# Per-channel attention kernel on one core: twelve e buffers, later column sums, halved T and y products, new order of loads and of the prologue

## Chip, cores, metric

One core of a Trainium2 chip (trn2) runs the whole program. The metric is the device time of one execution in microseconds (us).

## The reference, cut to what matters

x has the shape (8, 256, 32, 16): batch element, row, channel, column m. C_H is 256.

```python
n = group_norm(x)            # 8 groups over m (2 columns each); mean and variance over rows, channels, the group's columns
Q, K, V = W @ n + b          # over channels, for each (b, row, m): 32 -> 256; all stored as (B, S, 256, M)
QK = Q^T @ K                 # per (b, m): 256 x 256, summed over the 256 rows
A = softmax(QK, axis=-1)
out = einsum('bmcC,bmsC->bsCm', A, Vp)   # V weighted by the column sums of A
y = x + Wo @ out + bo
```

In the last einsum the letter c occurs only in A, so only the column sums of the softmax are needed: `a[C] = sum over c of A[c, C]`. And Q^T K depends on x only through the 32 x 32 Gram matrix of each (b, m) and the column sums of x.

## The kernel before

**Work.** An element is one b; it has 16 units m = 4t + q, four groups t of four units q. For an element the chain of statistics is: sums of rows (`sum_rows`, L361), group means (`mean`, L374), the rows centred on GpSimd (L910), the Gram matrix (`gram_of`, L382), the variance (`variance`, L400), the scaled Gram matrix `gnorm` (GpSimd, L941), its product with Wk for all four t (`t_product`, L410: 16 matmul calls into `bz` for even t and `by` for odd t) and with the bias (`tb_product`, L430), read out by VectorE (`read_t` L640, `read_tb` L651), split into a high and a low part (GpSimd L962, L985) and copied by DMA into `stack` (SyncE, L302).

**Softmax.** For each unit, TensorE computes a 256 x 256 score (`score`, L438: two halves into one of the four PSUM banks `s_bank`), VectorE the negated row maximum (`maximum`, L663), ScalarE two exponentials of 256 columns, each with its row sum (`exponentials`, L849), into one of `NE` = 8 buffers `e_sb`. After the four units of a group VectorE inverts the row sums (`invert`, L669) and TensorE adds the weighted columns into `acc` (`column_sums`, L454, in two halves h, 4 calls each). With 8 buffers ScalarE may begin group n + 2 only when the column sums of group n are done (L853).

**Output.** When an element's 16 units are done, `acc` is read (L673), turned into columns (`a_columns`, L468, bank `bx`; `read_a`, L678), multiplied into the output weights (GpSimd L997; `weights`, L479, bank `by`; `read_weights` and `read_bias`), and one element later `y_product` (L497: 16 calls into `bz` and `by`) is read by ScalarE (`read_even`, L860: two activations) and VectorE (`read_odd`, L699) and stored by SyncE (L325).

**Order.** The program is written in slots: slot 16b + p belongs to unit p of element b. Every engine runs its list in order, and waits are semaphores. In slot p TensorE first issues the score three units ahead (L536), VectorE the maximum two units ahead, ScalarE the exponentials of the unit itself. The column sums of group n stand at slots 4n + 5 and 4n + 6 (L542). The tables `ANCHOR`, `CHAIN`, `EARLY` (L42 to L52) place the statistics of element j, `OUT`, `OUT_FIRST`, `OUT_LAST` (L55 to L61) the output of the elements before. For element 5 on, seen from element b = j - 3 or j - 2: sum_rows slot 0, mean 3, Gram matrix 8, variance 13, then in the next element T product 3, its four reads 4 to 7, bias product 8 and its read 9. Weights stand at slot 13, their read at 15, the y product at 11 and its reads at 12. `BUSY` (L63) and `keep_busy` (L518, 4 calls a round) fill TensorE with products whose results nobody reads.

**Prologue** (L564 to L592, L787 to L821, L879 to L895, L1011 to L1034). SyncE loads the rows of elements 0 to 3, 512 KB each. ScalarE's queue loads the constants `k_sb` first, then Wk, the later constants `k2_sb`, bk, the stacked Wq, bv, bo, Wo and Wv; seven of these count on one semaphore, `w_loaded`, and the first T product (L577) and the splitting of Wq (L969) wait for all seven. `sum_rows` takes its matrix of ones from `k_sb`. Elements 0 and 1 are begun outside the slots; the first half of element 0's `stack` is copied as soon as t = 0 and 1 are split.

Of the kernel before, what the change touches and what calls it, by code (L numbers as in the profile page):

```python
# [8 lines left out]
CH = 256  # L9
G = 8  # L10
P = 128
# [15 lines left out]
ONES = PICK + M  # L27
LOMASK = ONES + C
# [13 lines left out]
ANCHOR = {2: 7, 3: 22, 4: 36, **{j: M * (j - 2) + 3 for j in range(5, B)}}  # L42
CHAIN = dict(
    sum_rows=-19, mean=-16, gram=-11, variance=-6, t_product=0, tb_product=5,
    sum_groups=-18, read_mean=-15, read_gram=-9, sum_diagonal=-8, read_variance=-5,
    read_t0=1, read_t1=2, read_t2=3, read_t3=4, read_tb=6,
)
EARLY = {
    2: {**CHAIN, **dict(gram=-7, variance=-4, read_gram=-6, sum_diagonal=-5, read_variance=-3)},
    3: {**CHAIN, **dict(sum_rows=-17, mean=-14, gram=-10, sum_groups=-16, read_mean=-13)},  # L50
    4: {**CHAIN, **dict(sum_rows=-18, mean=-15, sum_groups=-17, read_mean=-14)},
# [3 lines left out]
OUT = dict(read_acc=3, a_columns=5, read_a=6, weights=13, read_weights=15,  # L55
           y_product=11, read_even=12, read_odd=12)
OUT_FIRST = {**OUT, **dict(a_columns=7, read_a=8)}

OUT_LAST = dict(read_acc=3, a_columns=4, read_a=5, weights=8, read_weights=10,
                y_product=1, read_even=2, read_odd=3,  # L60
                y_second=12, read_even_second=13, read_odd_second=13)  # L61

BUSY = {(1, 3): 1, (1, 5): 1, (B - 1, 1): 2, (B - 1, 5): 2, (B - 1, 6): 1, (B - 1, 9): 1}  # L63
# [10 lines left out]
def shape_constants():  # L74
# [10 lines left out]
    k[:, ONES:ONES + C] = 1.0  # L85
# [15 lines left out]
def build(nc, x_rows, x_cols, wq_stack, wk_rep, bk_rep, wv, wo, bv, bo_rep, consts, later, y_cols):  # L101
# [7 lines left out]
    NE = 2 * Q  # L109
# [4 lines left out]
    with ctx:  # L114
# [23 lines left out]
        half = sb("half", [P, T])  # L138

# [43 lines left out]
        k_loaded = sem("k_loaded")  # L183
        k2_loaded = sem("k2_loaded")
# [31 lines left out]
        t_mm = sem("t_mm")  # L216
# [24 lines left out]
        y_mm = sem("y_mm")  # L241
        even_read = sem("even_read")
# [7 lines left out]
        def rows_of(eng, j):  # L250
            eng.wait_ge(xs_loaded[j], 16)
            return xs[:, j]
# [10 lines left out]
        def odd_t_bank(j):  # L263
            return {0: s_bank[0], 1: acc}.get(j, by)

        def odd_y_bank(j):
            return bx if j == B - 1 else by
# [21 lines left out]
        ones_m = k_sb[:, ONES:ONES + C]  # L289
# [5 lines left out]
        def _(sp):  # L295
# [29 lines left out]
            def store(j):  # L325
                sp.wait_ge(even_read, j + 1)
# [3 lines left out]
            for j in range(4):  # L330
                load_rows(j)
# [28 lines left out]
        def _(pe):  # L360
# [39 lines left out]
            def variance(j):  # L400
                pe.wait_ge(gram_done, j + 1)
                pe.wait_ge(trace_done, j + 1)
                if j == 0:
                    pe.wait_ge(k2_loaded, 16)
# [686 lines left out]
```

## Time and profile before

| | us |
|---|---|
| median of 3 runs (lowest, highest) | 184.82 (183.56, 187.84) |
| the profiled execution, its own time | 183.17 |
| its span, first to last instruction | 181.4 |
| busy: TensorE matmuls, VectorE, ScalarE, GpSimd | 153.9, 129.3, 127.9, 99.9 |
| mean granted TensorE clock | 0.979 of 2.4 GHz |

PE is TensorE, PEld its loading of weights, DVE VectorE, ACT ScalarE, POOL GpSimd, SP SyncE. L numbers are lines of the kernel before. Matmul ends are modelled, so a busy PE is not PE at its peak; intervals from start to start are firmer. One fp32 matmul call shows as two MATMUL records. The profiled execution is 1.65 us faster than the median of the three runs.

### The profile page before, as it was taken

What the parts mean: (1) busy time and instruction counts of PE and PEld (TensorE: products, weight loads), DVE (VectorE), ACT (ScalarE), POOL (GpSimd) and SP (SyncE); (2) the same over time, 40 slices, a digit from 0 to 9 for tenths busy, and PEclk for the clock granted to TensorE, in tenths of its full rate; (3) what the DMA queues carried; (4) which work ended last, traced back from release to release, by engine and by line L of the source; (5) the groups of instructions that cost most, each with busy time, mean ns of one, the idle gap of its engine ahead of it and who ended that gap; (6) DMA issues with size and microseconds to landing.
All of it is one profiled execution on the core that took longest, in us unless ns stands there. A gap on an engine that the chain in (4) does not pass through costs nothing. (4 is left out here: it accounts for less than half of the span.)

```text
span 181.4 us, 6452 instructions
## 1 busy us (share of the span) xinstructions
PE 153.9 (85%) x2448; PEld 87.1 (48%) x2448; DVE 129.3 (71%) x297; ACT 127.9 (71%) x529; POOL 99.9 (55%) x130
## 2 busy tenths in 40 slices
PE   6879797999978998899898979788978889899590
PEld 2254454555444655465545545544443445554340
DVE  0466899597778689767986798679778676668231
ACT  0200059789976798789688968897999998979301
POOL 3247739459975997685867595764742405125000
PEclk9996998799999999999999999999999999999999
DMA  5940859873992588099808870797077821200203
GB/s 179 409 157 4 202 150 176 187 241 54 206 226 114 101 213 268 21 176 230 301 5 160 193 243 4 129 215 250 4 150 169 264 90 41 116 4 5 116 4 116
DMA packets 10540, 26.72 MB, mean 147 GB/s; under 512 B 2603, under 2 KB 4110, under 8 KB 10510
## 3 DMA queue, kind: packets, MB, share of 16 engines
q1 hardware_dynamic: 8734, 25.25, 52.7%
q10 hardware_dynamic: 1776, 1.05, 2.0%
q8 instruction: 20, 0.33, 0.8%
q14 instruction: 10, 0.08, 0.2%
HBM read 9.13 MB, written 4.19 MB: 73 GB/s over the span
## 5 line engine op out<-in xcount | busy, mean ns | idle before, releaser
L855 ACT ACTIVATE e_sb<-s_bank,negmax 128x256 f32<-128x256 f32 x256 | 117.4, 491 | 33.9 <-DVE negmax L665 18.1
L665 DVE TENSOR_REDUCE negmax<-s_bank 128x2 f32<-128x512 f32 x128 | 85.8, 683 | 17.9 <-PE s_bank L450 16.6
L450 PE MATMUL s_bank<-stack,wq_st 99*128 99x256 f32 x256 | 57.3, 322 | 4.4 <-ACT e_sb L855 4.2
L855 ACT ACTIVATION_READ_ACCUMULATOR e_sb<-s_bank,negmax 128x1 f32 x256 | 57.3, 224 | 0.0
L450 PEld LDWEIGHTS s_bank<-stack,wq_st 99*128 99x128 f32 x256 | 37.0, 190 | 35.5 <-issue 35.1
L462 PE MATMUL acc<-e_sb,recip 128*32 128x256 f32 x512 | 41.4, 398 | 13.2 <-DVE recip L671 13.1
L462 PEld LDWEIGHTS acc<-e_sb,recip 128*32 128x32 f32 x512 | 10.6, 109 | 24.4 <-DVE recip L671 18.7
L1000 POOL TENSOR_TENSOR ws<-wo_sb,aT 128x1024 f32<-128x1024 f32 x7 | 13.4, 1910 | 13.5 <-DVE aT L681 13.5
L987 POOL TENSOR_TENSOR t_parts<-t_sb,t_parts 128x1280 fp32r<-128x1280 f32 x7 | 20.4, 2913 | 0.5
L916 POOL TENSOR_TENSOR xc<-xs,nm 128x512 f32<-128x512 f32 x12 | 12.3, 1043 | 7.4 <-DVE nm L619 7.4
L994 POOL TENSOR_TENSOR xcT<-xT,nmT 128x1024 f32<-128x1024 f32 x8 | 15.1, 1892 | 0.0
L865 ACT ACTIVATE yb<-bz,beff 128x256 f32<-128x256 f32 x16 | 6.7, 473 | 10.4 <-PE bx L514 7.6
L647 DVE SCALAR_TENSOR_TENSOR t_sb<-bk_sb,ssum,bz 128x256 f32<-128x256 f32 x16 | 7.6, 474 | 5.4 <-PE by L426 3.6
L939 POOL TENSOR_TENSOR rs<-vare,half 128x4 f32<-128x4 f32 x8 | 8.2, 1022 | 5.8 <-DVE vare L637 5.8
L1008 POOL TENSOR_TENSOR wf<-wn,k_sb 128x128 f32<-128x128 f32 x7 | 3.2, 455 | 14.8 <-DVE wn L688 14.8
L424 PE MATMUL bz<-wk_sb,gnorm 32*32 32x256 f32 x128 | 9.4, 406 | 0.5 <-DMA wv_sb<-wv 0.5
L933 POOL TENSOR_TENSOR gdiag<-gram,k_sb 128x128 f32<-128x128 f32 x6 | 2.6, 436 | 13.1 <-DVE gram L624 13.1
L512 PE MATMUL bz<-xcT,wf 32*32 32x256 f32 x128 | 8.7, 380 | 0.3 <-issue 0.3
L965 POOL CAST t_parts<-t_sb 128x1280 fp32r<-128x1280 f32 x6 | 7.5, 1250 | 2.0 <-DVE t_sb L654 2.0
L671 DVE RECIPROCAL recip<-rowsum 128x8 f32<-128x8 f32 x32 | 6.2, 194 | 2.1 <-ACT e_sb L855 2.1
L514 PE MATMUL by<-xcT,wf 32*32 32x256 f32 x112 | 7.6, 380 | 0.0
L609 DVE TENSOR_REDUCE part<-bx 128x4 f32<-128x256 f32 x7 | 2.8, 398 | 6.5 <-PE bx L369 6.4
(99 smaller groups left out, 180.9 us busy)
## 6 DMA issues: line engine op xcount, KB each, us to landing
stack<-t_parts SPq DMA_DIRECT2D x28, 256.0 KB, 5.0
stack<-t_parts SPq DMA_DIRECT2D x36, 128.0 KB, 4.6
xs<-x_rows SPq DMA_DIRECT2D x8, 512.0 KB, 5.4
xT<-x_cols SPq DMA_DIRECT2D x8, 512.0 KB, 5.5
y_cols<-yb SPq DMA_DIRECT2D x7, 512.0 KB, 3.6
y_cols<-yb SPq DMA_DIRECT2D x2, 256.0 KB, 2.6
stack<-t_parts ACTq DMA_DIRECT2D x4, 64.0 KB, 3.0
stack<-t_parts SPq DMA_DIRECT2D x4, 64.0 KB, 2.4
```

Source lines behind the costliest of these rows:

```text
L424: nc.tensor.matmul(bz[rows, cols], gnorm[rows, j % 2, 2 * i, :], wk_sb[rows, :], start=True, stop=True)
L450: mm = nc.tensor.matmul(s_bank[p % NS][:, CH * h:CH * h + CH], wq_st[:, P * h:P * h + P], stack[:, side, p % Q, p // Q, :], start=True, st ...
L462: mm = nc.tensor.matmul(acc[C * q:C * q + C, 0:CH], recip[:, t, q, h, :], e_sb[:, (Q * t + q) % NE, h, :], start=(t == 0 and h == 0), stop ...
L512: nc.tensor.matmul(bz[rows, cols], wf[rows, j % 2, 2 * i, :], xcT[rows, j % 2, 2 * i, :], start=True, stop=True)
L514: mm = nc.tensor.matmul(odd[across(q), cols], wf[rows, j % 2, 2 * i + 1, :], xcT[rows, j % 2, 2 * i + 1, :], start=True, stop=True)
L665: nc.vector.tensor_reduce(negmax[:, p % NS, :], s_bank[p % NS][:, :].rearrange("p (h n) -> p h n", h=HC), op=ALU.max, axis=AX.X, negate=Tr ...
L855: last = nc.scalar.activation(e_sb[:, p % NE, h, :], s_bank[p % NS][:, CH * h:CH * h + CH], ACT.Exp, bias=negmax[:, p % NS, h:h + 1], accu ...
L916: last = nc.gpsimd.tensor_tensor(xc[:, ch, :, 0:C].rearrange("p (g k) c -> p g k c", g=G), src[:, ch, :, :].rearrange("p (g k) c -> p g k ...
L939: nc.gpsimd.tensor_tensor(rs[:, j, :], vare[:, 0:T], half[:, :], ALU.pow).then_inc(rs_done, 1)
L987: nc.gpsimd.tensor_tensor(t_parts[:, j % 2, 1], t_sb[:, j % 2], t_parts[:, j % 2, 0].bitcast(f32), ALU.subtract).then_inc(parts_done, 1)
L994: nc.gpsimd.tensor_tensor(xcT[:, j % 2], xT[:, j], nmT[:, j, :, None].to_broadcast([P, T, S]), ALU.add).then_inc(xcT_done, 1)
L1000: nc.gpsimd.tensor_tensor(ws[:, :, :, :, :].rearrange("p h t q c -> p h (t q) c"), wo_sb[:, :, None, :].to_broadcast([P, HC, M, C]), aT[:, ...
```

## The change

- Twelve buffers `e_sb` (`NE` = 3Q), three sets of row sums; ScalarE waits at group n + 3 for the column sums of group n.
- The column sums of group n stand at slots 4n + 6 and 4n + 7.
- The T product and the y product are issued in halves (t = 0, 1 and t = 2, 3; 8 calls each) in neighbouring slots: T at slots 4 and 5, its reads at 6 (t = 1), 7 (t = 3), 8 (t = 0), 9 (t = 2), the bias product at 9 (it waits for two of the four reads only), its read at 11; y's first half at slot 13 with ScalarE's first read at 14, its second half at slot 0 of the next element, with ScalarE's second read at slot 1 and VectorE's at 2. In the last element they stand at slots 4, 5 and 12, 13.
- The weights (matmuls of L486 and L493) go to `bx`, the bank of the statistics and of `a`, at slot 12 with the read at 13; they wait for the read of the Gram matrix of element j + 4 instead of bank `by`. `variance` moves to 14, its read to 15, `sum_rows` to 1, `mean` to 4; in the element of the variance it waits for the bias read.
- `BUSY`: four rounds at slots 1, 2, 3 and 5 of element 0 are added (bank `by`); in the last element four rounds instead of six.
- Loads: the ones come from a memset. SyncE loads half of element 0's rows, then `k_sb`; ScalarE loads the other half, Wk, stacked Wq, `k2_sb`, bk and then the rest, with semaphores of their own for `k_sb`, Wk, Wq and bk. `w_loaded` counts the last four and is waited for by the product of Wo and bv and the first `a_columns`.
- Prologue: 3 rounds of `keep_busy` before the first `sum_rows`, which waits for the rows alone; T of element 0 in halves into four banks, the second half after the Gram matrix of element 1, with 6 rounds of `keep_busy` around where 3 were; `split_wq` before the first `power`.

```diff
-ANCHOR = {2: 7, 3: 22, 4: 36, **{j: M * (j - 2) + 3 for j in range(5, B)}}
+ANCHOR = {2: 8, 3: 22, 4: 36, **{j: M * (j - 2) + 4 for j in range(5, B)}}
-    sum_rows=-19, mean=-16, gram=-11, variance=-6, t_product=0, tb_product=5,
+    sum_rows=-19, mean=-16, gram=-12, variance=-6, t01_product=0, t23_product=1, tb_product=5,
-    read_t0=1, read_t1=2, read_t2=3, read_t3=4, read_tb=6,
+    read_t1=2, read_t3=3, read_t0=4, read_t2=5, read_tb=7,
...
-OUT = dict(read_acc=3, a_columns=5, read_a=6, weights=13, read_weights=15,
-           y_product=11, read_even=12, read_odd=12)
+OUT = dict(read_acc=4, a_columns=5, read_a=6, weights=12, read_weights=13,
+           y01_product=13, read_y0=14)
+OUT_NEXT = dict(y23_product=0, read_y2=1, read_odd=2)
...
-BUSY = {(1, 3): 1, (1, 5): 1, (B - 1, 1): 2, (B - 1, 5): 2, (B - 1, 6): 1, (B - 1, 9): 1}
+BUSY = {(0, 1): 1, (0, 2): 1, (0, 3): 1, (0, 5): 1, (1, 3): 1, (1, 5): 1,
+        (B - 1, 3): 1, (B - 1, 8): 1, (B - 1, 9): 1, (B - 1, 11): 1}
...
-    NE = 2 * Q
+    NE = 3 * Q
...
-            for j in range(4):
+            sp.dma_start(xs[:, 0, 0], x_rows[0, :, 0]).then_inc(xs_loaded[0], 16)
+            sp.dma_start(k_sb[:, :], consts).then_inc(k_loaded, 16)
+            for j in range(1, 4):
                 load_rows(j)
...
-                    pe.wait_ge(t_read, T * (j + 1))
+
+                    pe.wait_ge(t_read, T * j + 2)
...
-                    if slot >= Q + 1 and p % Q in (1, 2):
-                        n = (slot - Q - 1) // Q
-                        column_sums(n // T, n % T, p % Q - 1)
+                    if slot >= Q + 2 and p % Q in (2, 3):
+                        n = (slot - Q - 2) // Q
+                        column_sums(n // T, n % T, p % Q - 2)
...
-            keep_busy(s_bank[3], t_sb[:, 0, T, :], 4)
+            keep_busy(s_bank[3], t_sb[:, 0, T, :], 3)
+            sum_rows(0)
             pe.wait_ge(k_loaded, 16)
-            sum_rows(0)
...
-            pe.wait_ge(w_loaded, 16 * 7)
-            t_product(0)
+            pe.wait_ge(wk_loaded, 16)
+            t_product(0, 0, t01_mm)
+            keep_busy(s_bank[3], wk_sb, 1)
             tb_product(0)
             gram_of(1)
-            keep_busy(s_bank[3], wk_sb, 2)
+            t_product(0, 2, t23_mm)
+            keep_busy(s_bank[3], wk_sb, 3)
             variance(1)
             mean(2)
-            keep_busy(s_bank[3], wk_sb, 1)
-            t_product(1)
+            keep_busy(s_bank[3], wk_sb, 2)
+            t_product(1, 0, t01_mm)
+            t_product(1, 2, t23_mm)
...
                 if p % Q == 0:
-                    after(act, summed, T * b + p // Q - 1)
+                    after(act, summed, T * b + p // Q - NE // Q + 1)
...
-            act.dma_start(k_sb[:, :], consts).then_inc(k_loaded, 16)
-            act.dma_start(wk_sb[:, :], wk_rep).then_inc(w_loaded, 16)
+            act.dma_start(xs[:, 0, 1], x_rows[0, :, 1]).then_inc(xs_loaded[0], 16)
+            act.dma_start(wk_sb[:, :], wk_rep).then_inc(wk_loaded, 16)
+            act.dma_start(wq_raw[:, :], wq_stack).then_inc(wq_loaded, 16)
             act.dma_start(k2_sb[:, :], later).then_inc(k2_loaded, 16)
-            for dst, src in ((bk_sb, bk_rep), (wq_raw, wq_stack),
-                             (bv_sb, bv), (bo_sb, bo_rep)):
+            act.dma_start(bk_sb[:, :], bk_rep).then_inc(bk_loaded, 16)
+            for dst, src in ((bv_sb, bv), (bo_sb, bo_rep)):
                 act.dma_start(dst[:, :], src).then_inc(w_loaded, 16)
```

## Rows read from the trace of the kernel before

**Rows 1.** The page, part 1: busy us of each engine over the span

```profile
PE 153.9 (85%) x2448; PEld 87.1 (48%) x2448; DVE 129.3 (71%) x297; ACT 127.9 (71%) x529; POOL 99.9 (55%) x130
```

**Rows 2.** Windows per element: us; busy PE, PEld, DVE, ACT, POOL; granted clock; DMA share

```profile
23.55:42.34 18.79, 17.17 (x277) 9.85 (x277) 16.11 (x36) 15.15 (x64) 10.38 (x19) 0.91 0.69 171
42.34:61.27 18.93, 16.41 (x264) 9.84 (x263) 14.01 (x33) 15.23 (x64) 14.84 (x17) 1.00 0.65 148
61.27:79.97 18.70, 16.97 (x283) 10.33 (x283) 15.13 (x38) 15.85 (x67) 15.04 (x18) 1.00 0.68 162
79.97:98.53 18.56, 16.50 (x279) 9.97 (x279) 14.99 (x37) 15.85 (x67) 13.23 (x17) 1.00 0.68 174
98.53:117.10 18.57, 16.52 (x279) 9.97 (x279) 14.99 (x37) 15.85 (x66) 13.23 (x17) 1.00 0.61 146
117.10:134.49 17.39, 14.64 (x199) 8.08 (x199) 14.03 (x32) 15.71 (x67) 9.72 (x11) 1.00 0.64 155
134.49:150.84 16.35, 13.36 (x165) 7.53 (x165) 12.36 (x27) 15.63 (x67) 4.21 (x3) 1.00 0.60 175
150.84:168.24 17.40, 16.05 (x240) 8.34 (x239) 11.91 (x27) 15.40 (x65) 6.52 (x5) 1.00 0.08 32
```

**Rows 3.** Waits over the whole span: us in total, times, longest

```profile
ACT e_sb L855 <- PE acc L462: 15.7, 23, 1.4
PE acc L462 <- DVE recip L671: 13.1, 23, 1.9
```

**Rows 4.** Timeline of ACT: the first exponential of two units in a row

```profile
67.16 0.48 ACT L855 ACTIVATE e_sb<-s_bank,negmax 128x256 f32<-128x256 f32 x1
...
68.06 0.50 ACT L855 ACTIVATE e_sb<-s_bank,negmax 128x256 f32<-128x256 f32 x1
```

**Rows 5.** Timeline of PE in elements 4 and 5: start, us, records

```profile
108.14 0.38 PE L435 MATMUL by<-wk_sb,sblk 128*32 128x256 f32 x1 [0.18 <-DVE t_sb L647]
108.28 0.26 PE L395 MATMUL bx<-xc 128*32 128x33 f32 x6
...
109.24 0.50 PE L450 MATMUL s_bank<-stack,wq_st 99*128 99x256 f32 x2
109.68 0.64 PE L462 MATMUL acc<-e_sb,recip 128*32 128x256 f32 x8
110.25 0.50 PE L450 MATMUL s_bank<-stack,wq_st 99*128 99x256 f32 x2
...
111.68 0.40 PE L512 MATMUL bz<-xcT,wf 32*32 32x256 f32 x1
...
112.70 0.74 PE L450 MATMUL s_bank<-stack,wq_st 99*128 99x256 f32 x4
114.34 0.64 PE L462 MATMUL acc<-e_sb,recip 128*32 128x256 f32 x8 [0.89 <-DVE recip L671]
...
120.90 0.40 PE L424 MATMUL bz<-wk_sb,gnorm 32*32 32x256 f32 x1
...
126.30 0.59 PE L435 MATMUL by<-wk_sb,sblk 128*32 128x256 f32 x2 [0.19 <-DVE t_sb L647]
126.82 0.51 PE L450 MATMUL s_bank<-stack,wq_st 99*128 99x256 f32 x2
```

**Rows 6.** Timeline of the prologue

```profile
5.20 1.08 PE L369 MATMUL bx<-xs,k_sb 128*32 128x256 f32 x8 [0.19 <-DMA k_sb<-consts]
...
13.24 0.45 PE L424 MATMUL bz<-wk_sb,gnorm 32*32 32x256 f32 x1 [0.51 <-DMA wv_sb<-wv]
...
13.69 0.19 POOL L955 TENSOR_TENSOR ssum<-vare,rs 128x2 f32<-128x2 f32 x1
...
15.18 0.48 DVE L647 SCALAR_TENSOR_TENSOR t_sb<-bk_sb,ssum,bz 128x256 f32<-128x256 f32 x1 [1.50 <-PE s_bank L426]
```

**Rows 7.** A window of the prologue, with the columns of rows 2

```profile
12.00:16.00 4.00, 3.40 (x59) 1.45 (x61) 2.46 (x6) 0.00 (x0) 3.57 (x7) 0.68 0.01 4
```

**Rows 8.** Timeline of POOL in element 4: the power behind the statistics of element 7

```profile
116.33 1.02 POOL L939 TENSOR_TENSOR rs<-vare,half 128x4 f32<-128x4 f32 x1 [0.96 <-DVE vare L637]
```

More of the change, by code:

```diff
@@ L26 @@
 PICK = MEAN + 2 * P
[L27 to L28 removed]
+LOMASK = PICK + M
 OWN = LOMASK + 1
@@ L351, in _ @@
             store(B - 2)
-            for h, done in ((1, odd_read), (0, even_read)):
+            for h, done in ((1, odd_read), (0, y2_read)):
                 sp.wait_ge(done, B)
@@ L408, in variance, with t_product @@
                                  ).then_inc(var_mm, 1)
-            def t_product(j):
+            def t_product(j, first, done):
                 pe.wait_ge(gnorm_done, j + 1)
@@ L413, in t_product @@
                 after(pe, tb_done, j)
[L414 to L415 removed]
+                after(pe, y2_read, j - 4)
                 after(pe, odd_read, j - 4)
[L417 to L418 removed]
+                if j == 1:
                     pe.wait_ge(vare_done, 2)
[L420 to L428 removed]
+                even, odd, cols = t_bank(j, first), t_bank(j, first + 1), t_cols(j, first)
+                for q in range(Q):
+                    rows = slice(C * q, C * q + C)
+                    nc.tensor.matmul(even[rows, cols], gnorm[rows, j % 2, first, :], wk_sb[rows, :],
+                                     start=True, stop=True)
+                    mm = nc.tensor.matmul(odd[across(q), cols], gnorm[rows, j % 2, first + 1, :], wk_sb[rows, :],
+                                          start=True, stop=True)
+                mm.then_inc(done, 1)
             def tb_product(j):
@@ new lines, in element @@
+                    if (j := due("mean", slot)) is not None:
+                        mean(j)
+                    if last and p == at["y01_product"]:
+                        y_product(b - 2, 0, y01_mm)
+                    if last and p == at["y23_product"]:
+                        y_product(b - 2, 2, y23_mm)
+                    if (j := due("t01_product", slot)) is not None:
+                        t_product(j, 0, t01_mm)
+                    if (j := due("t23_product", slot)) is not None:
+                        t_product(j, 2, t23_mm)
@@ L640, in read_t @@
             def read_t(j, t):
-                dve.wait_ge(t_mm, j + 1)
+                dve.wait_ge(t01_mm if j == 0 and t < 2 else t23_mm, j + 1)
                 dve.wait_ge(ssum_done, j + 1)
@@ L746, in element @@
                         read_bias(b - 1)
-                    if b >= 2 and p == at["read_odd"]:
+                    if (j := due("read_variance", slot)) is not None:
+                        read_variance(j)
+                    if last and p == at["read_odd"]:
                         read_odd(b - 2)
```

216 lines of the change are left out of this document (109 added, 107 removed).

## Prediction

> **What bounds the kernel now.** I read the page first: no engine is busy all the time, and TensorE stands first with 153.9 us of a span of 181.4 [rows 1]. Then the span in one window per element [rows 2]: the eight elements take 144.7 us of it, the prologue before them 23.55 and the tail after the last exponential's start 13.2. In the elements the reader is to see three loads close together. ScalarE issues one unit (two exponentials with their row sums) every 0.90 us when nothing stops it [rows 4], 14.4 us for 16 units, and with the two reads of y (0.42 us each from start to start, an estimate from ScalarE's busy time of 15.85 against 15.23 without them) 15.3. TensorE is busy 16.5 us of 18.57 in elements 3 and 4, VectorE 15.0. Neither fills the element. The waits say why [rows 3]: ScalarE waits 15.7 us in 23 pieces for the column sums, and the column sums wait 13.1 us in 23 pieces for the inverted row sums, which come from ScalarE. That is a ring: with eight e buffers, group n + 2 may not begin before the column sums of group n, and these stand on TensorE two slots ahead of it, behind one score and whatever else the slot holds. When a slot holds a whole T or y product, the ring opens late. TensorE's in-order list waits in it too, so what it did not do then is late afterwards.
>
> So the present bound is the ring; behind it stands TensorE at 16.5, and behind that ScalarE at 15.3.
>
> **The change part by part.** Times are against the profiled execution (183.17, its span 181.4 and 1.8 around it).
>
> *Buffers and later column sums.* With twelve buffers the exponentials of group n + 3 wait for column sums that stand five slots earlier, at 0.9 us a slot 4.5 us ahead instead of 1.8. The longest wait there was 1.4 us [rows 3], so I take all 15.7 us of ScalarE's waits as gone. And the column sums, a slot later, find their reciprocals ready: the longest wait of PE was 1.9 us with 0.9 typical [rows 3, 5], one slot more and the loss of the ring cover it. What is late next is TensorE's own work, so this part gives an element not 18.57 - 15.3 but at most 18.57 - 16.5 = 2.05 us.
>
> *What the halves and new slots cost TensorE.* A score followed by other work takes 0.44 us from start to start (109.24 to 109.68), two in a row busy it 0.74 where two apart take 0.88; a half of the column sums takes 0.57; the whole y product 1.02 (111.68 to 112.70) [rows 5]. Half of 1.02 would be 0.51; the nearest group that stands between two scores, the half of the column sums, costs 0.57. So two halves cost 1.14, 0.12 more, for T as for y: 0.24. The bias product and the Gram matrix stood in one slot and took 1.10 together (108.14 to 109.24); apart they take 0.52 (126.30 to 126.82) and 0.96 (108.28 to 109.24), so 0.38 more. Four slots of a steady element held a score alone and now none does: four times 0.07, 0.3. The weights and the variance no longer stand in one slot: 0.1. Sum 1.0 us, bounds 0 (TensorE hides it all) and 1.8 (twice the halves and the separations, as the nearest groups show no such case). So a steady element needs 16.5 + 1.0 = 17.5 us of TensorE, and TensorE becomes the bound.
>
> The rule that speaks against the halves is in the Trainium skill, "TensorEngine Tiling (Array Packing)", section "Key Properties": "Changing tiling mode (not just tile) drains the TensorE". The scores use 99 x 128 weights, the others 32 x 32 or 128 x 32, so each of three new seams (in T, in y, between bias product and Gram matrix) brings two more changes. If only they cost something, at the 0.07 us by which a lone score is dearer than one of a pair [rows 5], the six come to 0.4 us an element in the place of 1.0, and the time to 172.5.
>
> *Element by element* [rows 2]. I add 0.25 us for waits that remain (a guess between 0 and the 2.05 of now), where TensorE bounds.
> - Element 0: 18.79. Four added rounds of matmuls at 0.57 are 2.3 us, of which PE's idle 1.6 covers most; the low clock in it (0.91 on average) may go (up to 1.7 us of work saved) or stay. I take half: 18.3, gain 0.5.
> - Element 1: 16.41 busy, plus the halves of T, lone scores and separations 0.8, plus 0.25: 17.5, gain 1.45.
> - Element 2: 16.97 busy; y's second half leaves it (-0.5), +1.0 + 0.25: 17.7, gain 1.0.
> - Elements 3 and 4: 17.8, gain 0.75 each.
> - Element 5: TensorE needs 14.64 + 0.6 = 15.2, so ScalarE's 15.3 + 0.3: gain 1.8.
> - Element 6: 15.3 + 0.2, gain 0.85.
> - Element 7 (to the start of its last exponential): 16.05 busy, two rounds fewer (-1.1), y's half from before (+0.57), halves of two products (+0.25), a little wait: 16.2, gain 1.2. ScalarE there: 15 intervals of 0.90 and five reads, 15.6.
>
> Sum of gains 8.3 us. Edits I cost at nothing: the weights in `bx` at slot 12 (GpSimd has its products for them early in the element, it waits for the next step in between); the statistics' waits moved by a slot; VectorE's 15.0 us lie under 17.5, but leave only 0.3 under ScalarE's pace in elements that reach it; ScalarE's read of y at slot 14 must wait for a product issued one slot before, up to 1 us, which it makes good at 0.90 us a unit against TensorE's 1.1. SyncE's copies of `stack` for element b + 2 are issued more than half an element before they are needed; only those for element 1 have less, as element 0 gets shorter, and they move with the prologue.
>
> *Prologue.* The first product waited for `k_sb` until 5.20 [rows 6]; now it needs the rows alone, which come as the first load on both queues with half of the bytes on each. An estimate: 0.6 us earlier (0 to 0.9). The first T product waited 0.5 us for the last weight (to 13.24), and its first read (15.18) 1.5 us for all 16 calls, most of them at the low clock, 0.68 in that window [rows 6, 7]. The read also needs `ssum`, done at 13.88 [rows 6]; with the first half read by itself it can start right there. So this path ends 1.3 us earlier, plus the 0.6: 1.9. Against that the later constants and bk now lie behind more bytes on their queue, and the second half of T of element 0 comes later on. From the first split the SyncE queue is the bound up to the first scores, which moves as a whole; but the first score also stands behind element 1's bias product, whose chain gains the 0.6 and some of the rest. I take 1.6; bounds -0.5 (the later constants arrive last and the clock stays low) and 2.4.
>
> *Tail.* The last y product in halves: +0.12 for TensorE, while ScalarE reads one part early. VectorE's read of both odd parts is what the stores wait for, so 0 (bounds -0.4, +0.4).
>
> Sum: 183.17 - 8.3 - 1.6 = 173.3 against the profiled execution. The median of three runs stands 1.65 above that, so 174.9 on the scale of the runs.
>
> **The rivals.**
> 1. *The halves are free* (or the low clock goes for good): TensorE stays at 16.5 in elements 1 to 4, four times 1.0 us more gain and another 0.7 from element 0: about 170. For: matmul records overlap heavily. Against: a score alone takes 0.44, in a pair 0.37, and the bias product alone 0.52 [rows 5].
> 2. *ScalarE's pace everywhere*: if TensorE's busy time is no floor at all, elements 0 to 4 come to about 15.4: 18.2 us gained there in the place of 4.5, and 161 to 163. The rows speak against it: between waits TensorE's groups start back to back at 1.00 us for a score and half a column sum [rows 5], and these alone are 8 of the 16.5. A sentence of the Trainium skill speaks for it, in "Trainium Kernel Development and Optimization", section "Performance Expectations": matmul busy time is called a bad metric for the distance to the roofline, since matmuls are pipelined.
> 3. *The ring goes, but an in-order wait takes its place*: TensorE waits in slots 4, 5, 8 or 14, where three groups stand in a slot and VectorE's or ScalarE's part comes one slot behind it. If half of the 2.05 us of idle time stays, elements 1 to 4 give 0.8 us less each and 5 to 7 half of theirs, 1.9: 174.9 + 3.2 + 1.9 = 180.
> 4. *Slower*: T is read two slots later (11 instead of 9), so GpSimd's split of it (1.25 + 2.9 us) ends later and with it the power behind the next variance, the scaled Gram matrix and the T product at slot 4. Now the power starts at 116.33 [rows 8] and the T product at 120.90 [rows 5]; the power and two scalings fill about 1.6 us of that, so 3 us are free, and one slot has been added to T's place. If the delay came to more than 3 us, TensorE would stand still at slot 4 of five elements; each us beyond costs 5 us in all, and from 2 us beyond the whole gain is gone: with 2.5 beyond, 174.9 + 12.5 = 187. Against it: GpSimd waited 0.96 us for the variance in the row itself [rows 8], and is busy 13.2 of 18.6.
>
> **How the numbers follow.** My sum 0.56 (172.5 to 178), rival 1 0.13, rival 2 0.03, rival 3 0.23, rival 4 0.05. The range 168.5 to 181.0 leaves out rival 2, rival 4 and the far end of rival 3, some 2 in 10. A measurement of this kernel tells about 2% from no change, here 181.1: my sum, rivals 1 and 2 and two thirds of rival 3 lie under it, 0.88; within 2% 0.08; slower 0.04.
>
> **What would show it.** In the waits, the line of ScalarE waiting for the column sums should be under 2 us, and that of the column sums for the reciprocals under 4. In windows by element, elements 3 and 4 should take 17.3 to 18.0 with PE busy over 17, elements 5 and 6 near 15.5. The first exponential should start near 22.0. If elements 3 and 4 come to 16.5 or less, the cost of the halves is wrong; if they stay above 18.2 with TensorE idle over 1 us, rival 3 holds, and the waits name the place; if TensorE waits for `gnorm` at the T product, rival 4.

## The result and the profile after

The changed kernel took 180.99 us in the median of four runs (178.03 to 183.55), the kernel before 184.61 beside it. The ratio is 0.967, with a 95% interval of 0.959 to 0.976: faster by 3.3%, where I forecast 5.4% against 184.8. It compares the fast runs alone, 178.03 and 178.43 against three of the kernel before between 183.56 and 184.82; the medians of all runs are 2.0% apart. The median lies 0.01 us under the top of my range (181.0), and two of the four runs lie above the range: that the number fell inside is luck.

The profiled execution took 183.55 us, its span is 181.5, and it is one of those with a long stretch in which TensorE was granted half its clock. Busy times and idle time of the main groups, from the page (line, operation, count, busy us, mean ns, idle before and what ended it):

```profile
PE 167.0 (92%) x2480; PEld 88.7 (49%) x2480; DVE 130.1 (72%) x297; ACT 129.1 (71%) x529; POOL 100.1 (55%) x131
...
L880 ACT ACTIVATE e_sb<-s_bank,negmax 128x256 f32<-128x256 f32 x256 | 117.5, 497 | 22.1 <-DVE negmax L692 21.9
...
L475 PE MATMUL acc<-e_sb,recip 128*32 128x256 f32 x512 | 43.8, 419 | 0.8 <-DVE recip L698 0.8
```

ScalarE's 15.7 us of waiting for the column sums [rows 3] are gone, and the column sums wait 0.8 us for reciprocals where it was 13.1. The windows by element, with the prologue last, answer to [rows 2]:

```profile
core 0: us, PE busy (x) PEld busy (x) DVE busy (x) ACT busy (x) POOL busy (x), PEclk, DMA share, GB/s
23.83:40.84 17.01, 17.01 (x292) 9.14 (x291) 15.20 (x34) 15.27 (x64) 9.27 (x18) 1.00 0.75 192
40.84:59.15 18.31, 17.53 (x276) 10.30 (x275) 14.79 (x37) 15.63 (x64) 13.63 (x16) 1.00 0.60 148
59.15:76.53 17.38, 16.83 (x263) 9.41 (x263) 14.89 (x35) 15.57 (x65) 16.13 (x18) 1.00 0.69 166
76.53:94.10 17.57, 17.57 (x280) 9.69 (x280) 15.04 (x35) 15.99 (x68) 13.29 (x17) 1.00 0.71 184
94.10:111.66 17.56, 17.56 (x280) 9.69 (x280) 15.04 (x35) 15.99 (x68) 13.29 (x17) 1.00 0.64 156
111.66:127.66 16.00, 15.60 (x205) 8.17 (x204) 13.96 (x31) 15.53 (x69) 9.91 (x12) 1.00 0.67 165
127.66:146.39 18.73, 18.03 (x163) 9.33 (x162) 12.39 (x25) 15.51 (x68) 5.67 (x5) 0.68 0.55 139
146.39:168.01 21.62, 20.60 (x248) 9.49 (x248) 12.54 (x26) 16.33 (x68) 6.11 (x4) 0.81 0.13 50
...
0.00:23.83 23.83, 18.86 (x348) 9.97 (x348) 12.46 (x35) 1.28 (x2) 12.77 (x30) 0.93 0.59 188
```

What is to be seen: elements 3 and 4 take 17.57 and 17.56 us (18.56 and 18.57 before), and TensorE is busy in all of it. Elements 6 and 7 are longer than before, at a granted clock of 0.68 and 0.81. And the prologue is no shorter. Windows inside elements 6 and 7 show when the clock fell:

```profile
127.60:131.00 3.40, 3.18 (x39) 1.40 (x39) 2.72 (x6) 3.40 (x16) 2.92 (x3) 1.00 0.92 195
131.00:134.30 3.30, 2.86 (x24) 1.95 (x28) 3.17 (x9) 3.30 (x17) 0.52 (x2) 1.00 0.96 211
134.30:138.00 3.70, 3.70 (x23) 1.88 (x17) 1.68 (x3) 3.70 (x18) 1.83 (x1) 0.50 0.97 282
...
150.00:154.80 4.80, 4.80 (x38) 2.04 (x30) 2.56 (x5) 4.12 (x17) 1.89 (x1) 0.50 0.29 113
```

From 134.3 to 154.8 us TensorE ran at 1.2 GHz. The fall comes 6.6 us into element 6, which has the least work for TensorE (163 records against 280 in element 4).

The prologue, TensorE's first products:

```profile
4.17 0.81 PE L383 MATMUL bx<-xs,ones 128*32 128x256 f32 x8
8.47 1.08 PE L383 MATMUL acc<-xs,ones 128*32 128x256 f32 x8 [2.31 <-DMA xs<-x_rows]
10.49 1.08 PE L409 MATMUL bx<-xc 128*32 128x33 f32 x64
...
14.13 0.40 PE L436 MATMUL bz<-wk_sb,gnorm 32*32 32x256 f32 x1
```

The first row sums start at 4.17 instead of 5.20 [rows 6], as meant. But then TensorE waits 2.31 us for the rows of element 1, which its list wants before element 0's Gram matrix, and the first T product starts at 14.13 instead of 13.24. During that wait the granted clock fell to half, from 8.0 to 11.4 us: the row sums and the Gram matrix behind it took 1.08 us each, where 0.64 and 0.76 are their times at full rate.

### The profile page after: what moved, and what is told of

The parts are those of the page before. It is cut to its first block and busy times, and to the rows that moved or that the text cites. A ratio compares the mean times of both kernels' runs of the same rounds, so it can differ in the third digit from the quotient of the medians.

```text
span 181.5 us, 6548 instructions
## 1 busy us (share of the span) xinstructions
PE 167.0 (92%) x2480; PEld 88.7 (49%) x2480; DVE 130.1 (72%) x297; ACT 129.1 (71%) x529; POOL 100.1 (55%) x131
## 5 line engine op out<-in xcount | busy, mean ns | idle before, releaser
L692 DVE TENSOR_REDUCE negmax<-s_bank 128x2 f32<-128x512 f32 x128 | 87.0, 686 | 23.8 <-PE s_bank L463 22.8
L463 PE MATMUL s_bank<-stack,wq_st 99*128 99x256 f32 x256 | 64.7, 343 | 1.1 <-ACT e_sb L880 1.0
L463 PEld LDWEIGHTS s_bank<-stack,wq_st 99*128 99x128 f32 x256 | 40.2, 201 | 43.2 <-issue 42.3
L880 ACT ACTIVATION_READ_ACCUMULATOR e_sb<-s_bank,negmax 128x1 f32 x256 | 58.6, 229 | 0.0
L475 PE MATMUL acc<-e_sb,recip 128*32 128x256 f32 x512 | 43.8, 419 | 0.8 <-DVE recip L698 0.8
L475 PEld LDWEIGHTS acc<-e_sb,recip 128*32 128x32 f32 x512 | 10.7, 111 | 10.8 <-issue 1.8
L522 PE MATMUL bz<-xcT,wf 32*32 32x256 f32 x128 | 11.3, 415 | 1.8 <-ACT yb L889 1.8
L524 PE MATMUL by<-xcT,wf 32*32 32x256 f32 x128 | 11.4, 417 | 0.0
L533 PE MATMUL s_bank<-wk_sb 32*32 32x256 f32 x128 | 8.7, 379 | 0.0
L438 PE MATMUL by<-wk_sb,gnorm 32*32 32x256 f32 x96 | 7.9, 386 | 0.0
L730 DVE TENSOR_TENSOR yb<-by,beff 128x512 f32<-128x512 f32 x8 | 5.5, 683 | 3.3 <-PE by L524 3.3
```

Of the source, the lines that this page charges most:

```text
L463: mm = nc.tensor.matmul(s_bank[p % NS][:, CH * h:CH * h + CH], wq_st[:, P * h:P * h + P], stack[:, side, p % Q, p // Q, :], start=True, st ...
L475: mm = nc.tensor.matmul(acc[C * q:C * q + C, 0:CH], recip[:, t, q, h, :], e_sb[:, (M * b + Q * t + q) % NE, h, :], start=(t == 0 and h == ...
L522: nc.tensor.matmul(bz[rows, cols], wf[rows, j % 2, first, :], xcT[rows, j % 2, first, :], start=True, stop=True)
L524: mm = nc.tensor.matmul(by[across(q), cols], wf[rows, j % 2, first + 1, :], xcT[rows, j % 2, first + 1, :], start=True, stop=True)
L533: nc.tensor.matmul(dst[rows, 0:CH], src[rows, 0:C], src[rows, 0:CH], start=True, stop=True)
L692: nc.vector.tensor_reduce(negmax[:, p % NS, :], s_bank[p % NS][:, :].rearrange("p (h n) -> p h n", h=HC), op=ALU.max, axis=AX.X, negate=Tr ...
```

## The experiments

Where elements are compared, it is in profiles in which their clock is full. The kernel before ran beside them between 181.3 and 203.0 us, with granted clocks from 0.995 down to 0.839, so times of single variants say less than their windows do.

**1. The changed kernel again.** No edit.

> The changed kernel once more. Theory A (the ring is gone, TensorE bounds elements 2 to 4, and what the last two elements lost comes from a half clock in them): elements 3 and 4 take 17.5 to 17.6 us whatever the clock does later, and the spread of the runs (178.0 to 183.6) is the length of the low-clock stretch in elements 6 and 7. A profile with a short stretch shows element 7 shorter and elements 0 to 5 the same within 0.3 us. Rival (the spread comes from the loads or the prologue): the first exponential's start moves by as much as the whole time does.

Measured: 177.69 us in the median (174.30 to 178.24). Elements 3 and 4, then 6 and 7 of its profile:

```profile
77.79:95.36 17.57, 17.57 (x280) 9.71 (x280) 15.04 (x35) 15.99 (x69) 13.30 (x17) 1.00 0.73 185
95.36:112.92 17.56, 17.56 (x280) 9.71 (x280) 15.03 (x35) 15.99 (x69) 13.29 (x17) 1.00 0.63 156
128.91:144.20 15.29, 13.94 (x168) 7.51 (x167) 12.51 (x25) 15.29 (x69) 5.68 (x5) 1.00 0.67 171
144.20:161.89 17.69, 16.64 (x243) 8.01 (x246) 12.38 (x25) 16.12 (x67) 6.10 (x4) 1.00 0.16 62
```

With a full clock element 6 takes 15.29 and not 18.73, element 7 17.69 and not 21.62: 7.4 us that the half clock had cost. Elements 0 to 5 are the same within 0.02 us. Here the prologue had the stretch: the first exponential started at 25.09 instead of 23.83. So both theories hold a part: the end and the prologue each make spread.

Element 1 takes 18.3 us here as in the first profile, where I had forecast 17.5. One wait in it is GpSimd's. The centred rows stand behind 1.89 us of its other work and are ready at 54.00, and TensorE's list stands at a Gram matrix until then:

```profile
51.96 2.04 POOL L947 TENSOR_TENSOR xc<-xs,nm 128x512 f32<-128x512 f32 x2
54.11 0.76 PE L409 MATMUL bx<-xc 128*32 128x33 f32 x64 [0.62 <-issue]
```

**2. Filling rounds in element 6.**

```diff
+        (B - 2, 4): 1, (B - 2, 5): 1, (B - 2, 8): 1, (B - 2, 9): 1, (B - 2, 12): 1,
```

> The changed kernel with five rounds of filling matmuls in element 6 (slots 4, 5, 8, 9, 12), where TensorE has least to do. Theory A (TensorE's light load in element 6 lets its clock fall to half, and elements 6 and 7 then pay for it): granted clock 1.00 through elements 6 and 7, element 6 at 15.5 to 16 us, element 7 at 16 to 17, the whole 5 to 8 us faster than the 183.55 of the profiled execution of the changed kernel, about 175. Rival (the fall of the clock is chance or has another cause): the stretch at half clock stays, and the time is that of the changed kernel or up to 1 us more for the five rounds.

Measured: 177.28 us (175.14 to 179.57). The clock was full in elements 6 and 7, but so it was in run 1 without the rounds, and element 6 took 16.53 us, 1.24 more than there. What makes the clock fall in element 6 stays open; the rounds are no gain. The prologue of this profile ran at half rate up to element 0's Gram matrix and at full rate behind it:

```profile
7.26 1.08 PE L384 MATMUL acc<-xs,ones 128*32 128x256 f32 x8
9.28 1.11 PE L410 MATMUL bx<-xc 128*32 128x33 f32 x64
```

The rows of element 1 landed at 7.22 here and held nothing up. The exponentials began at 22.67, 0.9 us under the 23.55 of before. Run 3, with the prologue of before, began them at 23.29 with TensorE at full rate from its first row sums on; so the new prologue gave 0.6 us although its own start was slower. What it gives at equal rate no pair of profiles shows.

**3. Twelve buffers alone, in the kernel before.** The edits to `NE`, `rowsum`, `e_sb` and ScalarE's wait, nothing else.

> The kernel before with twelve e buffers and three sets of row sums alone; slots, halves, banks and prologue as before. Theory A (the ring through eight buffers was the bound): ScalarE's waits for the column sums fall from 15.7 us to under 2, TensorE's own work with whole T and y products, 16.5 us, becomes the floor of elements 1 to 4, and they take 16.8 to 17.6; the whole gains 5 to 9 us. Rival (the column sums also have to stand a slot later, since TensorE waits 13.1 us in its own list for the reciprocals): elements stay at 18 us and more, the gain is under 3 us and TensorE's waits for the reciprocals stay over 8 us.

Measured: 186.47 us, ratio 1.018 (1.013 to 1.023). The waits, and elements 3 and 4:

```profile
PE acc L462 <- DVE recip L671: 15.7, 24, 1.8
```

```profile
77.51:96.08 18.57, 16.47 (x279) 9.97 (x278) 14.99 (x35) 15.90 (x69) 13.25 (x16) 1.00 0.69 175
96.08:114.64 18.56, 16.46 (x279) 9.96 (x278) 14.99 (x35) 15.88 (x68) 13.24 (x16) 1.00 0.59 146
```

No wait of ScalarE for the column sums is left in the list, and elements 3 and 4 are as long as before. Elements 2 and 5 are longer (19.43 and 17.84 against 18.70 and 17.39), and the tail holds a stretch at half clock (16.4 us). The rival was right: TensorE, in its own list, waits for reciprocals one slot too early, 15.7 us in all, where it was 13.1.

**4. Eight buffers in the changed kernel.**

```diff
-    NE = 3 * Q
+    NE = 2 * Q
```

> The changed kernel with eight e buffers in the place of twelve, all else changed. Theory A: the ring is back and tighter, since the column sums stand a slot later: ScalarE waits at every group for them, elements 3 and 4 take 19 to 20 us, the whole is 5 to 12 us slower than the changed kernel. Rival (the halves and the new slots did the work, the buffers little): within 2 us of the changed kernel.

Measured: 223.76 us (202.53 to 241.16); elements 3 and 4 take 18.50 each, and the wait is back in the list:

```profile
ACT e_sb L880 <- PE acc L475: 35.9, 30, 5.4
```

The ring is there; in a steady element it costs 0.94 us and not the 2 I expected. Most of the rest is time at half clock: the profile has about 53 us of it (mean clock 0.868), 44 of them in one stretch that begins in element 6, and the three slower runs have mean clocks down to 0.675. Why this kernel falls so often is open.

**5. Twelve buffers and the later column sums, in the kernel before.**

```diff
-                    if slot >= Q + 1 and p % Q in (1, 2):
-                        n = (slot - Q - 1) // Q
-                        column_sums(n // T, n % T, p % Q - 1)
+                    if slot >= Q + 2 and p % Q in (2, 3):
+                        n = (slot - Q - 2) // Q
+                        column_sums(n // T, n % T, p % Q - 2)
```

> The kernel before with twelve buffers and the column sums one slot later; whole T and y products, banks, slots of the output and prologue as before. With the buffers alone ScalarE no longer waited for the column sums, but TensorE waited 15.7 us for reciprocals and elements 3 and 4 stayed at 18.56. Theory A (the later slot is the other half of opening the ring): TensorE's wait for reciprocals falls under 4 us and elements 3 and 4 come to 16.8 to 17.6, by the cost of the missing seams below the 17.56 of the changed kernel; the whole near 175. Rival (a whole y product with ScalarE's read one slot behind it stalls ScalarE for over 1 us, and with it everything behind): the elements stay at 18 us or more, and the waits of ScalarE's y read and of the maximum take the place of the ones removed.

Measured: 178.06 us (176.02 to 182.22), ratio 0.976 (0.960 to 0.993). Elements 3 and 4, and the waits of the column sums:

```profile
81.91:99.54 17.63, 16.94 (x283) 10.04 (x282) 14.78 (x36) 15.88 (x68) 12.95 (x17) 1.00 0.71 183
99.54:117.17 17.63, 16.93 (x283) 10.02 (x282) 14.78 (x36) 15.88 (x69) 13.21 (x17) 1.00 0.63 154
```

```profile
PE acc L462 <- DVE recip L671: 2.1, 1, 2.1
```

With runs 3 and 4 this is nearly a square: steady elements of 18.56 with neither edit, 18.56 with the buffers alone, 18.50 with all but the buffers, 17.63 with the two alone and 17.56 with the whole change. The later column sums alone were not run; run 4 has them together with the halves and banks. The two edits together are the gain in the steady element. The halves, the new banks and slots add 0.07, and theory A's guess that run 5 would come in under the changed kernel was wrong. That 0.07 is a balance of two larger terms. Here TensorE is idle 0.7 us of an element, and 0.5 of it is waiting for reads of the bank `by`:

```profile
109.21 0.38 PE L435 MATMUL by<-wk_sb,sblk 128*32 128x256 f32 x1 [0.25 <-DVE t_sb L647]
...
114.59 0.64 PE L486 MATMUL by<-ws,wv_sb 128*32 128x128 f32 x16 [0.27 <-DVE yb L703]
```

The change takes both waits away (the bias product waits for two reads only, the weights go to `bx`) and fills the time with the seams that run 6 prices. Even without halves TensorE is busy 16.94 us here and not 16.50.

**6. Fewer seams in the changed kernel.**

```diff
-    sum_rows=-19, mean=-16, gram=-12, variance=-6, t01_product=0, t23_product=1, tb_product=5,
+    sum_rows=-19, mean=-16, gram=-12, variance=-6, t01_product=0, t23_product=0, tb_product=4,
```

> The changed kernel with both halves of T in slot 4 and the bias product in slot 8 with the Gram matrix, the reads where they are. It measures the cost of the seams. My estimate: 0.12 us for the seam in T and 0.38 for the one between Gram matrix and bias product, so elements 3 and 4 fall from 17.56 to about 17.1, elements 1 to 4 save 2 us together. Rival (seams are free, TensorE's busy time counts only overlap): 17.56 stays. Second rival (a fuller slot brings a stall elsewhere): over 17.56.

Measured: 175.93 us (174.67 to 177.66). Elements 3 and 4:

```profile
79.60:96.50 16.90, 16.90 (x280) 9.62 (x280) 14.70 (x35) 15.95 (x68) 13.24 (x17) 1.00 0.74 191
96.50:113.41 16.91, 16.91 (x280) 9.63 (x280) 14.70 (x35) 15.96 (x68) 13.26 (x17) 1.00 0.66 162
```

The same 280 records take 0.66 us less. That is what the two seams cost together, where I had 0.12 and 0.38; the run doesn't tell them apart. The Trainium skill ("TensorEngine Tiling (Array Packing)", "Key Properties") has a drain at each change of tiling mode; the direction agrees. If the whole 0.66 were drains, the four changes of mode would cost about 0.16 us each (an estimate), twice the 0.07 that I had put in; no run parts a drain from the other effects of a seam. With run 5, the rest of the change (halves of y, banks, the freed waits) is worth 17.63 - 16.90 = 0.73 us, and the halves of T with the bias product apart give 0.66 of it back. Elements 1 to 4 save 1.6 us together and not 2: element 1 saves 0.03, since TensorE's wait for the centred rows grows there to 1.21 us.

**7. Element 0's Gram matrix first.** `sum_rows(1)` behind `gram_of(0)`, `mean(1)` behind `variance(0)`, and VectorE's reads likewise.

> The changed kernel with the row sums and the mean of element 1 behind the Gram matrix of element 0, on TensorE and VectorE. Theory A (the new order of loads brings element 1's rows later, and TensorE's in-order list held element 0's Gram matrix behind them, 2.3 us of waiting in the profile): the first T product starts 1 to 2 us earlier against the first product of the row sums than in the changed kernel, and the first exponential starts 0.5 to 1.5 us earlier at the same clock. Rival (the path to the first exponential goes through element 1, or through the copies of stack, so nothing is won): the first exponential starts at 22.7 at full clock as with the five filling rounds.

Measured: 174.96 us (173.91 to 177.44). Its prologue:

```profile
4.25 1.08 PE L383 MATMUL bx<-xs,ones 128*32 128x256 f32 x8
8.66 0.74 PE L409 MATMUL bx<-xc 128*32 128x33 f32 x63 [1.22 <-DVE xc L782]
...
11.33 0.64 PE L383 MATMUL bx<-xs,ones 128*32 128x256 f32 x8
```

The Gram matrix starts at 8.66 (10.49 in the changed kernel, 9.28 in run 2) and waits now for the centred rows; the first exponential starts at 21.62, 1.05 us ahead of run 2. How much of it is the order is open: TensorE is at full rate from the Gram matrix on here (64 records in 0.76 us; 1.11 in run 2). Run 9, with the same order and a Gram matrix at half rate, came to 22.69, as run 2 did, though element 1's rows landed at 8.1 there and at 7.2 in run 2. So the order takes the late rows off the path, and against run 2, whose rows were not late, the 1.05 us are the clock's as far as these profiles show.

**8. The loads of before.** Rows of element 0 whole on SyncE's queue, `k_sb` first on ScalarE's.

> The changed kernel with element 0's rows whole on SyncE's queue and the constants first on ScalarE's, as before the change; Wq, the later constants and bk as in the change. Theory A (splitting the rows brings the first row sums 1 us earlier but element 1's rows 1.5 us or more later): first row sums at 5.0 to 5.2 instead of 4.2, element 1's rows at 6.6 to 7.0 instead of 8.4, and the Gram matrix of element 0 no later than 9.4 instead of 10.5; the first exponential 0.3 to 1 us earlier than in the changed kernel at the same clock. Rival (the split is what gains): the first exponential 0.6 us or more later.

Measured: 176.79 us (174.03 to 178.87). Its prologue:

```profile
4.96 1.08 PE L381 MATMUL bx<-xs,ones 128*32 128x256 f32 x8 [0.75 <-DMA xs<-x_rows]
7.92 1.08 PE L381 MATMUL acc<-xs,ones 128*32 128x256 f32 x8
9.94 1.11 PE L407 MATMUL bx<-xc 128*32 128x33 f32 x64
14.30 1.08 PE L381 MATMUL bx<-xs,ones 128*32 128x256 f32 x8 [0.35 <-DVE vare L663]
```

The second row sums wait for no load, and the Gram matrix starts at 9.94, not at 9.4 or before, since TensorE runs at half rate here; its first exponential starts at 26.10. The fair partner is run 6, whose prologue is that of the changed kernel and runs at half rate too: 26.85. So here before's order of loads is 0.75 us better with the list as it is; the split wins 0.8 us at the first row sums and loses more at the second. But that hangs on one landing: in run 6 the rows of element 1 came at 8.53. In run 2, also at half rate up to there, they came at 7.22, and the Gram matrix started at 9.28, 0.66 us before this run's. So the split loses in the one pair, where these rows land late, and wins in the other. Of the ten profiles with the new order of loads four have the rows by 7.9, when the second row sums of this run start.

These two prologues show the spread of the starts: the clock column has 1.00 in all of their windows, but the durations say otherwise. In run 6:

```profile
14.94 1.08 PE L383 MATMUL bx<-xs,ones 128*32 128x256 f32 x8 [0.35 <-DVE vare L665]
```

Eight records that take 0.64 us in run 7 take 1.08. The Trainium skill has it in "TensorE: Matmul & The Clock Gate", Part 1: "the default state is throttled, and activity releases the throttle". The traces agree: the 24 filling records ahead of the first row sums take 2.78 us in every profile of the changed kernel and its variants, and 24 such records take 1.50 at full rate (run 11). The first full rate comes between 4 us and, in run 6, 20.6 us, five before the first score.

**9. Both wins together** (6 and 7).

> The changed kernel with both edits that won by themselves: T's halves in one slot and the bias product beside the Gram matrix, and element 1's row sums behind element 0's Gram matrix. Theory A (the two act in different stretches and TensorE's own work bounds the steady elements): elements 3 and 4 at 16.9 us as with the first alone, the first exponential at 21.6 us at full clock as with the second alone, the whole about 171 to 172 us where the clock is full in the prologue. Rival (they share a gain): the whole stays at the 174.7 to 175 us of either.

Measured: 173.18 us over six runs (172.29 to 184.34), ratio 0.943 (0.936 to 0.951). Elements 3 and 4 take 16.9 us each, so the first win is whole; the median is 1.8 us under run 7's and 2.8 under run 6's. The first exponential starts at 22.69 and not at 21.6, with the Gram matrix at half rate, as run 2 had it without the second edit. So the second win doesn't show in this profile.

**10. Without three filling rounds in the last element.**

```diff
-        (B - 1, 3): 1, (B - 1, 8): 1, (B - 1, 9): 1, (B - 1, 11): 1}
+        (B - 1, 3): 1}
```

> The same combination without the filling rounds at slots 8, 9 and 11 of the last element (the one at slot 3 stays). Theory A (the last element took 17.7 us and not 16.2 because TensorE is behind there: three rounds at 0.57 us stand ahead of the second y product, and ScalarE waits 1.5 us for it): the interval of 2.87 us at slot 13 falls to under 1.9, the last element to 16.2 to 16.7, the whole gains 1 to 1.5 us. Rival (the rounds keep the clock): a stretch at half clock appears in the last element or the tail, and the time is the same or worse.

Measured: 174.16 us over seven runs (170.56 to 176.58). The last element takes 15.81 us instead of 17.69: no idle time is left ahead of ScalarE's read of y. The lowest run is 1.7 us under run 9's, the median is not. In this profile the prologue was at half clock from 8.6 to 15.5 us (first exponential 23.66) and element 1 had a stretch too (19.38); the four other slower runs have no profile.

**11. More filling where TensorE waits for centred rows.**

```diff
-            keep_busy(s_bank[3], k_sb, 1)
+            keep_busy(s_bank[3], k_sb, 3)
```

> The same combination with three filling rounds instead of one between the first mean and the first Gram matrix, where TensorE waits 2 us for the centred rows. Theory B (the late first exponentials, 25 to 27 us in three profiles against 21.6 to 22.7 in two, are prologues in which TensorE still runs at half clock, and the idle time ahead of the Gram matrix decides it): row sums of element 2 take 0.64 us and not 1.08 in the profile, the first exponential starts by 22 us, and the slowest of the runs is within 2 us of the fastest. Rival (it is chance at every start, and the filling changes nothing or delays the Gram matrix by up to 0.8 us): the spread of the runs stays at 3 to 4 us.

Measured: 172.59 us, six runs between 172.40 and 173.25. The first exponential starts at 21.50. The filling records and the Gram matrix behind them:

```profile
6.68 1.50 PE L533 MATMUL s_bank<-k_sb 32*32 32x256 f32 x24
8.53 0.74 PE L409 MATMUL bx<-xc 128*32 128x33 f32 x63 [0.35 <-DVE xc L782]
```

The spread of 0.85 us against 6 in run 10 speaks for theory B. Against run 9 it says less: five of its six runs lie within 1.9 us, and the sixth, 184.34, has a mean clock of 0.907, about 34 us at half rate, more than the prologue is long. And the filling didn't bring the full rate in this profile: the mean's records at 6.14 us run at it already (0.61 us for four, 1.02 at half rate), before the two added rounds. It may have held it, where run 10's prologue lost it again at 8.6. Six runs of one kernel do not exclude chance.

**12. Both.**

> The combination with three filling rounds ahead of the first Gram matrix and without the three in the last element. Theory A (the two are independent: one holds the clock in the prologue, the other only delayed TensorE's list): the first exponential at 21.5 us, elements 3 and 4 at 16.9, the last element at 15.8 where it was 17.7, the whole 1.9 us under the 172.6 of the combination with the filling, 170.5 to 171, all runs within 1.5 us. Rival (the last element's rounds hold the clock for the last element and the tail): some runs 2 us or more slower, with a stretch at half clock behind 145 us.

Measured: 171.18 us, six runs between 170.00 and 172.27. The windows: prologue, elements 3 and 4, element 7, tail; then the filling and the Gram matrix:

```profile
0.00:23.18 23.18, 20.78 (x364) 10.91 (x364) 12.46 (x35) 1.28 (x1) 12.83 (x30) 1.00 0.61 195
76.01:92.93 16.92, 16.92 (x280) 9.64 (x280) 14.70 (x35) 15.96 (x68) 13.26 (x17) 1.00 0.74 191
92.93:109.84 16.91, 16.91 (x280) 9.63 (x279) 14.69 (x35) 15.96 (x68) 13.25 (x17) 1.00 0.66 162
140.91:156.71 15.80, 14.76 (x219) 7.48 (x222) 12.11 (x25) 15.80 (x68) 6.11 (x4) 1.00 0.17 69
156.71:170.20 13.49, 7.41 (x152) 3.50 (x144) 3.78 (x9) 1.96 (x7) 0.00 (x0) 0.91 0.22 79
...
7.24 2.79 PE L533 MATMUL s_bank<-k_sb 32*32 32x256 f32 x24
9.96 1.01 PE L409 MATMUL bx<-xc 128*32 128x33 f32 x64
```

The last element holds at 15.80 with a full clock. The first exponential is at 23.18 here: with the filling in place the prologue ran at half rate up to the Gram matrix, so the filling does not bring the full clock. At half rate the three rounds take 2.79 us and put the Gram matrix at 9.96, where run 9 had it at 8.96, and the first exponential 0.5 us later than there. The spread is 2.3 us where I expected 1.5, the median 171.18 just above the expected 170.5 to 171. This version is faster than both kernels: 6.5 us under the changed kernel's median in run 1, and 10 under the lowest run of the kernel before (181.25).

## Why the prediction was right or wrong

**The bound (right, by half of its reason).** I said the ring of eight buffers bounds the kernel and TensorE's own work stands behind it. Runs 3 to 5 show that the ring has two links: freeing the first (the buffers) alone is worth nothing in a steady element, and all the rest without it 0.06 us. My step "the column sums find their reciprocals ready" I had costed as a detail of the buffers; it is half the cause.

**The steady element (right in its total, partly by luck in its terms).** Forecast 17.5 of work plus 0.25 of waits, measured 17.56 with no idle time. I had all of the added 1.0 us as the cost of halves, lone scores and separations. The two seams of run 6 are dearer than I had them (0.66 against 0.50). Another 0.44 is there in run 5 without any half; my 0.3 for lone scores may be a part of it, the rest is a term I didn't have. The halves of y and the moved weights then add almost nothing where I had 0.2. That TensorE's records form a floor (against rival 2) is supported by run 6: the same records, 0.66 us less, and still 100% busy. For ScalarE I said 15.3 and run 1's element 6 took 15.29, but my working there doesn't hold together: 15.85 against 15.23 is 0.31 a read and not 0.42.

**Element by element, with a full clock** (the changed kernel, elements 6 and 7 from run 1), gains forecast and measured against the profile before, in which 3.4 us of element 0 are at half clock, us:

| element | 0 | 1 | 2 | 3 | 4 | 5 | 6 | 7 | sum |
|---|---|---|---|---|---|---|---|---|---|
| forecast | 0.5 | 1.45 | 1.0 | 0.75 | 0.75 | 1.8 | 0.85 | 1.2 | 8.3 |
| measured | 1.8 | 0.6 | 1.3 | 1.0 | 1.0 | 1.4 | 1.1 | -0.3 | 7.9 |

The sum holds, some terms do not, and their errors cancel. Element 0 gained 1.3 us more; its clock stayed full, and of the up to 1.7 us that this is worth I had taken half. Element 1 gained 0.8 less: TensorE was busy 17.53 us where I had 17.2, and idle 0.78 where I had 0.25, most of that in front of the Gram matrix that waits for GpSimd's centred rows (run 1). Element 7 lost: I counted two filling rounds fewer, but not that three of the four stand right ahead of the second y product, in slots 8, 9 and 11; run 10 gives 1.9 us back without them, and 15.8 is 0.2 above what I had computed for ScalarE alone (15.6).

**The prologue (wrong in size).** I took 1.6 us. In run 2, the best profile with the change's order of work, it is 0.9, and in the two profiles of the changed kernel nothing or less. The part behind the first T product came nearly as forecast: from its start to the first exponential runs 2, 7, 9, 11 and 12 take 9.7 us, and run 3, with the old prologue and a full clock, 10.8 (my 1.3 for reading the first half early). The step that failed is the first 0.6, up to the T product: I followed the rows of element 0 and the constants, and did not ask when the rows of element 1 would then land and what stood behind them in TensorE's list. The first row sums came 1.03 us earlier, but the late rows held the second by 2.31 us and the Gram matrix behind them, and the T product started at 14.13 instead of 13.24. Run 7 takes these rows off the path. Run 8 against run 6 and run 2 shows both sides: the old order of loads is better by 0.65 us at the Gram matrix when the rows land at 8.5, worse by 0.66 when they land at 7.2.

**The tail (at its bound).** Forecast 0 with +0.4 as its bound; 13.5 us in the profiles of the changed kernel and of the variants that have its tail (13.6 in run 4), against 13.1 before and in run 5.

**The clock (a missing term).** Prologue, elements and tail without the stretches give 183.17 - 7.9 - 0.9 + 0.4 = 174.8, near my 173.3; the lowest run was 174.30. What is above it is in the profiles time at half clock: 8.6 us in elements 6 and 7 and the prologue of the first profile, 2.4 in the prologue of run 1's. I had the clock only in element 0 and in one bound of the prologue, as if the two short stretches of the profile before were a property of the kernel. They differ from run to run, for the kernel before too (181.3 to 203.0). The median of 180.99 comes from two runs with the long stretch (183.55 both, mean clock 0.926) and two with less of it (178.03 and 178.43, 0.96); in run 1 the changed kernel's median was 177.69.

**The rivals.** Rival 1 fell with run 6: the halves are not free. Rival 2 fell with the steady element at 17.56; its price was added up wrongly, since elements 0 to 4 come from 93.55 to 77.0 us at 15.4 each, 16.6 and not 18.2, and the time to about 163. Rival 3 (another in-order wait takes the place) is what the buffers alone do (run 3). In the changed kernel the nearest to it is element 1's wait of 0.62 us. Rival 4 fell: over the whole span the T product waits 0.2 us for `gnorm`, and elements 3 and 4 hold no idle time of TensorE at all.

## What to carry to other kernels

When two engines wait for each other in a ring, look at both links, the buffers and the place in the in-order list; freeing one can be worth nothing and both together the whole gain. When a load is brought forward, ask which one goes back and what stands behind it in the list. Filling rounds belong where the engine waits anyway; ahead of work that another engine waits for they cost time (1.9 us for three rounds at 0.57 us here). A price from one pair of profiles is a price at one landing time and one clock: look for a second pair before you call an order of loads better.

## What the runs showed of the hardware that I had not expected

- The clock column can show 1.00 while matmuls run at half rate: eight row-sum records took 1.08 us in the prologues of runs 6 and 8 and 0.64 at full rate, and the window of 12 to 19 us has 1.00 in both. Durations are the surer sign at the start of an execution.
- A stretch at half clock came in element 6 of the changed kernel. In the 3.30 us before it TensorE was busy 2.86 us and had no idle gap over 0.35 us. It lasted 20.5 us although TensorE then showed busy nearly all the time. The same kernel kept its full clock there in another profile.
- Element 1's rows (512 KB) landed between 7.2 and 8.7 us in the changed kernel's order, from profile to profile, where they landed at 6.55 to 6.66 in the four profiles with the order of before. Element 0's rows landed at 4.0 to 4.2 instead of 4.9 to 5.1.
